# Twenty pairs of destinations per burst of counts, in a three-layer graph network on one core

## What is computed

```python
def _mean_agg(x, src, dst, n):
    msg_sum = segment_sum(x[src], dst, num_segments=n)
    cnt = segment_sum(ones, dst, num_segments=n)
    return msg_sum / maximum(cnt, 1.0)

def _sage_conv(x, src, dst, Wl, bl, Wr):
    return _mean_agg(x, src, dst, x.shape[0]) @ Wl.T + bl + x @ Wr.T

h = relu(_layernorm(x))
h = relu(_batch_norm(_sage_conv(h, src, dst, Wl0, bl0, Wr0), gamma0, beta0))
h = relu(_batch_norm(_sage_conv(h, src, dst, Wl1, bl1, Wr1), gamma1, beta1))
return x + log_softmax(_sage_conv(h, src, dst, Wl2, bl2, Wr2))
```

## Time and profile before

| | |
|---|---|
| median of 3 runs | 1584.37 us (1583.73 to 1584.45) |
| the profiled execution | 1584.4 us, span 1582.6 us |
| PE busy, share of the span | 1403.9 us (89%) |
| PEld busy | 1125.9 us (71%) |
| DVE busy | 559.7 us (35%) |
| ACT busy | 541.1 us (34%) |
| POOL busy | 639.2 us (40%) |
| block 0 of layer 0 | 0 to 63.5 us |
| blocks 1 to 24 of layer 0 | 63.5 to 545 us |

### The profile page before, as it was taken

How to read it: one execution, slowest core, us unless ns; L and a number is a source line. 1 busy time by engine, 2 the same in 40 slices (tenths; PEclk the granted TensorE clock), 3 DMA queues, 4 the chain that set the end, 5 groups by cost and what they waited for, 6 DMA issues and landing times. The chain is left out here.

```text
span 1582.6 us, 37175 instructions
## 1 busy us (share of the span) xinstructions
PE 1403.9 (89%) x16601; PEld 1125.9 (71%) x16601; DVE 559.7 (35%) x1023; ACT 541.1 (34%) x906; POOL 639.2 (40%) x636
## 2 busy tenths in 40 slices
PE   1499999999999999888988988988988898999997
PEld 0377777777777788666766766766766886788886
DVE  6968686868777632000010100001000211212223
ACT  4887878787877654000000000000000330000001
POOL 4332222222222000666566566566562004666640
PEclk9999999999999999999999999999999999999998
DMA  5254545454545427555555556455551367898992
GB/s 154 87 187 174 183 176 180 168 183 170 189 165 198 178 55 276 172 169 191 189 171 210 170 171 212 154 170 177 200 167 46 108 234 271 296 327 292 315 315 81
DMA packets 83896, 298.02 MB, mean 188 GB/s; under 512 B 17680, under 2 KB 53026, under 8 KB 70508
## 3 DMA queue, kind: packets, MB, share of 16 engines
q1 hardware_dynamic: 51900, 225.46, 39.8%
q0 software_dynamic: 25408, 65.24, 13.6%
q10 hardware_dynamic: 6424, 4.88, 1.0%
HBM read 204.30 MB, written 91.22 MB: 187 GB/s over the span
## 5 line engine op out<-in xcount | busy, mean ns | idle before, releaser
L1132 PE MATMUL bank<-ring,parts 128*128 128x250 f16 x6664 | 825.7, 274 | 41.3 <-issue 35.1
L1132 PEld LDWEIGHTS bank<-ring,parts 128*128 128x128 f16 x6664 | 624.5, 98 | 154.6 <-issue 65.2
L500 POOL DMA_INDIRECT hots<-table,src_i x518 | 492.9, 951 | 510.0 <-DMA table<-parts 204.1
L636 ACT CAST ring<-cells 128x980 f16<-128x980 f32 (+1 forms) x325 | 335.4, 1058 | 109.6 <-PE cells L1124 97.9
L1132 PE MATMUL cells<-ring,parts 128*128 128x250 f16 x1960 | 241.5, 276 | 27.4 <-issue 26.5
L864 DVE TENSOR_TENSOR hots<-iotas,tab 128x980 f16<-128x980 f16 (+3 forms) x262 | 245.4, 995 | 10.3 <-ACT tab L600 10.3
L1132 PEld LDWEIGHTS cells<-ring,parts 128*128 128x128 f16 x1960 | 190.2, 99 | 71.3 <-issue 49.2
L1669 ACT ACTIVATE Z<-bank,vec 128x250 f32<-128x250 f32 x48 | 20.0, 468 | 432.8 <-PE bank L1150 249.9
L1124 PEld LDWEIGHTS cells<-hots 64*128 64x128 f16 x4670 | 80.4, 96 | 95.6 <-issue 50.4
L1124 PE MATMUL cells<-hots 64*128 64x49 f16 x4670 | 107.2, 186 | 42.5 <-DVE hots L864 34.7
L452 POOL DMA_INDIRECT rows_i<-in_dst_rows_dram,row_i x25 | 36.3, 1453 | 192.4 <-DVE row_i L729 186.6
(11 more groups left out here) (199 smaller groups left out, 845.8 us busy)
## 6 DMA issues: line engine op xcount, KB each, us to landing
c_blocks<-ring SPq DMA_DIRECT2D x25, 3062.5 KB
ring<-c_blocks SPq DMA_DIRECT2D x39, 1562.5 KB
ring<-c_blocks SPq DMA_DIRECT2D x39, 1500.0 KB
rcb<-rc_row SPq DMA_DIRECT2D x68, 125.0 KB
hots<-table,src_i POOLq DMA_INDIRECT x518
Z<-in_x_dram SPq DMA_DIRECT2D x4, 768.0 KB, 7.5
table<-parts SPq DMA_DIRECT2D x2, 1536.0 KB
table<-parts ACTq DMA_DIRECT2D x2, 1536.0 KB
```

The source lines that it names most:

```text
L500: pool.indirect_dma_start(out=got[layer][:, 5 * (r % NGOT) + i, :], out_offset=None, in_=tables[layer], in_offset=bass.IndirectOffsetOnAxi ...
L636: act.copy(blk[c % 2][:, :, :].rearrange("p a (d g) -> p a d g", d=GD)[:, :, :, GPS * i:GPS * i + n], cells[t % 2][:, :, 0:n * NA].rearran ...
L1132: return pe.matmul(bank[b][:, 0:BD], view[0:r, a, part, m * P:m * P + P], blk[s][0:r, a, :], start=(a, part) == (0, 0), stop=(a, part) == ...
```

## The change

In `pe_layer0` the counts of two steps (i and i + 1, with i even) are issued in a run, 40 matmuls, ahead of all other work of the two steps; the sums of both steps follow, with the turns, the linear matmuls and the transposes at their places among them. The last step of a block stays alone. In `act_layer0` all of ScalarE's other work of a step moves into a function `act_chores(c, i)`, and is issued for both steps after the evictions of both. The work itself, the tiles, the semaphores and the lists of VectorE, GpSimd and SyncE are the same.

```diff
+        def act_chores(c, i):
+
+            t = NST * c + i
+            what, q, b = chores.get(t, ("", 0, 0))
...
+            if 1 <= c <= NG and i == 10:
+                a0, n, r = groups[c - 1]
+                w = (n - 1) * P + r
+                act.wait_ge(t_h0, c)
+                act.activation(Z[:, 0, P * a0:P * a0 + w], bank[7][:, 0:w], ACT.Relu).then_inc(a_h0, 1)
+
         def act_layer0():
...
                         act.copy(blk[c % 2][:, :, :].rearrange("p a (d g) -> p a d g", d=GD)[:, :, :, GPS * i:GPS * i + n],
                                  cells[t % 2][:, :, 0:n * NA].rearrange("p d (g a) -> p a d g", g=n)).then_inc(a_cells, 1)
-                    what, q, b = chores.get(t, ("", 0, 0))
...
-                        act.activation(Z[:, 0, P * a0:P * a0 + w], bank[7][:, 0:w], ACT.Relu).then_inc(a_h0, 1)
+                    if i % SPH == SPH - 1 or i == NST - 1:
+                        for k in range(i - i % SPH, i + 1):
+                            act_chores(c, k)
             act_last(0)
...
                 for i in range(NST):
                     t = NST * c + i
-                    if c < NB:
-                        pe_cells(c, i)
+                    if c < NB and i % SPH == 0:
+                        for k in range(i, min(i + SPH, NST)):
+                            pe_cells(c, k)
                     what, q, b = chores.get(t, ("", 0, 0))
                     if what == "turn":
                         pe_turn(q, b)
```

More of the change, by code:

```diff
@@ L619, in act_relu @@
             act.copy(small[0:r, a0:a0 + n, 0, :], X[0:r, a0:a0 + n, :]).then_inc(a_hi0, 1)
+        def act_chores(c, i):
+            t = NST * c + i
+            what, q, b = chores.get(t, ("", 0, 0))
+            if what == "sample":
+                act_sample(b)
+            elif what == "row":
+                act_row(q, b)
+            elif what == "turn":
+                act_turn(q, b)
+            if t == 1:
+                for b in range(*batches[1]):
+                    act_row(1, b)
+            elif t == 3:
+                act.wait_ge(v_lnvar, 1)
+                act.activation(rsx[:, 1, :], rsx[:, 2, :], ACT.Sqrt, bias=epsc[:, 0:1]).then_inc(a_lnstd, 1)
+            if t == TG - 24:
+                act.wait_ge(v_base, 1)
+                junk_wait()
+                act.activation(junk[0:W, 0:R], smp_i[0:W, :], ACT.Sign, bias=base[0:W, 4:5], scale=-1.0,
+                               accum_out=s1[0:W, NB:NB + 1]).then_inc(a_gsample, 1)
+                junked.append(a_gsample)
+            elif t == TG - 11:
+                act.wait_ge(d_grow, 16)
+                junk_wait()
+                act.activation(junk[0:W, 0:256], grow[0:W, :], ACT.Sign, bias=base[0:W, 4:5], scale=-1.0,
+                               accum_out=s2[0:W, NB:NB + 1]).then_inc(a_ginrow, 1)
+                junked.append(a_ginrow)
+            elif t == TG + 1:
+                act.wait_ge(d_gwin, 16)
+                act.activation(gloc[0:W, :], gloc[0:W, :].bitcast(I32), ACT.Identity,
+                               bias=base[0:W, 3:4]).then_inc(a_gconv, 1)
+            elif t == TG + 4:
+                act.copy(gsrc[0:W, :], gsrc[0:W, :].bitcast(I32)).then_inc(a_gconv, 1)
+            elif t in (TG + 8, TG + 11):
+                act_group_count((t - TG - 8) // 3)
+            if t in ln_at and ln_at[t] in act_groups:
+                act_relu(ln_at[t])
+            if c >= 2 and i == 6:
+                b = c - 2
+                act.wait_ge(t_lin, b + 1)
+                if b == 0:
+                    act.wait_ge(p_lo, len(act_groups))
+                    act.wait_ge(v_lo, len(vec_groups))
+                for m in range(2):
+                    act.activation(Z[:, m, BD * b:BD * b + BD], bank[7][:, BD * m:BD * m + BD], ACT.Identity,
+                                   bias=bias[0][:, m:m + 1]).then_inc(a_z, 1)
+            if 1 <= c <= NG and i == 10:
[3 more added lines that the diff above has]
+                act.activation(Z[:, 0, P * a0:P * a0 + w], bank[7][:, 0:w], ACT.Relu).then_inc(a_h0, 1)
@@ L637, in act_layer0 @@
                                  cells[t % 2][:, :, 0:n * NA].rearrange("p d (g a) -> p a d g", g=n)).then_inc(a_cells, 1)
-                    what, q, b = chores.get(t, ("", 0, 0))
-                    if what == "sample":
-                        act_sample(b)
-                    elif what == "row":
-                        act_row(q, b)
-                    elif what == "turn":
-                        act_turn(q, b)
-                    if t == 1:
-                        for b in range(*batches[1]):
-                            act_row(1, b)
-                    elif t == 3:
-                        act.wait_ge(v_lnvar, 1)
-                        act.activation(rsx[:, 1, :], rsx[:, 2, :], ACT.Sqrt, bias=epsc[:, 0:1]).then_inc(a_lnstd, 1)
@@ L682, in act_layer0 @@
-                    if 1 <= c <= NG and i == 10:
-                        a0, n, r = groups[c - 1]
-                        w = (n - 1) * P + r
-                        act.wait_ge(t_h0, c)
-                        act.activation(Z[:, 0, P * a0:P * a0 + w], bank[7][:, 0:w], ACT.Relu).then_inc(a_h0, 1)
+                    if i % SPH == SPH - 1 or i == NST - 1:
+                        for k in range(i - i % SPH, i + 1):
+                            act_chores(c, k)
             act_last(0)
```

31 lines of the change are left out of this document (removed).

## The result

The changed kernel takes 1591.69 us (median of 5 runs, 1586.92 to 1593.54) where the kernel before takes 1583.93 (5 runs beside it, 1582.31 to 1584.45): a ratio of 1.0046, 95% interval 1.0029 to 1.0063. It is slower by 7.8 us. The forecast was 1573.9, its range ended at 1586. The profiled execution of the changed kernel has 1591.69 us, its span 1589.8 us, so 7.2 us more than the span before, and a mean granted clock of 0.973, as before.

A forecast was written before the change was run, and what follows sets the result against it. TensorE was taken to bound blocks 1 to 24 of layer 0, ScalarE close behind. A saving of 31.3 us less 20.8 of added waiting left 10.5: 1584.4 - 10.5 = 1573.9 us, range 1560 to 1586.

The forecast's parts named there:

- x: Time of the second 20 count loads in a pair's run of 40 on TensorE: 0.26 us, bounded by 0.21 and 0.33.
- gross gain: TensorE's saving before new waits: 144 pairs at 0.20 us plus 23 gaps at 0.11 after linear matmuls, together 31.3 us.
- The rival with two gaps in a burst: The 0.21 us gap belongs to each step's own start, so nothing is saved and new waits are paid: 1595 us, chance 0.08.
- margin of a plain pair: With ScalarE doing evictions only, TensorE reaches the next burst's second half at 2.70 us, ScalarE frees it at 2.68: nothing lost.
- ScalarE sets the pace everywhere: Rival: evictions pitched at 1.06 us make every plain pair wait 0.07, 10 us in 144: 1584 us, chance 0.17.
- new waits: TensorE's added waiting, mainly for ScalarE's other work after its slack of 0.86 us is spent: 20.8 us in all.
- Turns: Step 11's turn waits for step 10's copy, now after both evictions: 0.9 to 1.3 us instead of 0.25, 0.9 more a batch.
- Samples: ScalarE's sample work at pair (10, 11), step 12 and pair (0, 1) makes TensorE wait 2.3 us, against 1.3 before.
- Rows: Row searches on ScalarE: covered when alone; two in pair (0, 1) make TensorE wait 0.55 us.
- The copy to Z: ScalarE's copy in each block makes TensorE wait 0.28 us, three times a batch 0.8; nothing before.
- The clock: Rival: longer waits drop TensorE's clock, costing 1.4 us a drop; one at each of fifteen places gives 1595 us, chance 0.07.
- ScalarE's lag: Rival: the lag is caught up elsewhere and only half of the added waiting comes: taken as 1562 us, chance 0.16.

The follow-up runs named there:

- e17: Kernel before, with evictions copying half their columns from block 2 on and the block store in seven column pieces; ratio 0.9927 to the kernel before.
- e18: Changed kernel, with evictions copying half their columns from block 2 on and the block store in seven column pieces; ratio 0.9762 to the kernel before.
- e13: Kernel before, with the block store in seven column pieces, one at each of steps 0 to 6 of the next block; ratio 0.9999 to the kernel before.
- e14: Changed kernel, with the block store in seven column pieces, one at each of steps 0 to 6 of the next block; ratio 0.9970 to the kernel before.
- e9: Kernel before, with blocks 1 to 24 storing only one of 49 column groups; ratio 0.9987 to the kernel before.
- e10: Changed kernel, with blocks 1 to 24 storing only one of 49 column groups; ratio 0.9957 to the kernel before.

## Why the prediction was wrong

The sum of what the change gives held. x, the second 20 loads, is 0.26 as taken (40 in 0.59 or 0.60), 15 sums take 1.51 (forecast 1.52), one gap of 0.21 stands for each pair, and plain pairs take 2.35 to 2.37 us where they do not wait. The gross gain is 27.5 to 30 us in e17 and e18 for 31.3. The rival with two gaps in a burst is refuted, and by the same rows the rule of the Trainium skill that a weight load is pulled ahead (TensorE: Matmul & The Clock Gate, on loading the stationary operand) does not cover this switch: 0.21 us stands at each pair, as it did at each step.

Two steps failed.

First, **the list of rivals had no place for TensorE's own instructions**. The prediction says "SyncE's, GpSimd's and VectorE's lists do not move" and that their work "costs nothing as long as TensorE is behind it", and looked at waits on semaphores only. Stops behind instruction packets grew by 18.4 us (1.4 to 19.8) and blocks 1 to 24 by 9.8, so the rest of the change gave 8.6. Where no stop is left it gives 3.8 (e13 and e14) or 5.3 (e9 and e10); the other 3 to 5 us must be waits that a stop took the place of, and only 2 of them are seen (26.0 us of waits for ScalarE against 28.1 in e14). The stops were in the trace of before, 1.4 us of them, and were passed by as noise. So was the margin, at n = 43 1.4 us between the late packet and TensorE. The Trainium skill's page Runtime: NRT & Kernel Launch, Instruction fetch mechanics, describes the blocks of 16 KiB, 256 instructions each, and calls the cost of crossing a boundary "mostly hidden"; the trace agrees on the 256, and has the cost hidden before, and not after. The Trainium skill's page DMA: Bandwidth & Descriptors, Queues, rings and completion order, says that a DMA engine goes round its queues by whole packets of some 9 to 17 descriptors. How many descriptors a row of the store makes no run shows; the trace has the instruction packet between two rows, after six of eight at 357.69, and not behind all of the engine's share.

Second, **the margin of a plain pair**. The step reads: "It comes there, at the second half of the next burst, at 2.37 + 0.33 = 2.70", against 2.68 for the eviction. But the same prediction had just taken 0.26 for the second 20 and so, by the same slope, for the first 20 of an unbroken run: the second half starts 0.26 after the first, at 2.63. The run of 40 that takes 0.67 in place of 0.59 is that wait. In e18 against e17 the median pair gains 0.20 or 0.21 at every place. In e14 against e13 it gains that only at step 6, behind the linear matmuls, and 0.14 at step 0, 0.12 at step 2, 0.08 at step 4, 0.14 at step 8; at step 10 it loses 0.07. The rival "ScalarE sets the pace everywhere" had the mechanism, with 0.17 for its chance and the wrong reason (an eviction's pitch of 1.06; it is 0.97: the row at 351.17 has two in 2.05). The Trainium skill's warning in TensorEngine Tiling (Array Packing), PSUM Bottleneck, is borne out: with evictions halved the pairs are worth 23.9 us, with whole ones 3.8.

The size of the new waits, forecast at 20.8 us, comes out at 31.3 - 3.8 = 27.5 with the stops away. It lies in the middle of the bursts: the 144 runs of 40 loads take 37.4 us more than 0.59 each in e14, and 3.6 in e18. A part of it has no term in the forecast at all: eight evictions of e14 and seven of the changed kernel start 0.46 to 0.50 us late with no releaser that the trace can name, and TensorE waits for them (0.86 us at 344.73 in the changed kernel); the cause is open. Turns had 0.9 to 1.3 us forecast at step 11's; in block 16 of the changed kernel it was 1.31, ScalarE's copy after both evictions just as described:

```profile
392.23 2.03 ACT L689 CAST ring<-cells 128x980 f16<-128x980 f32 x2
...
394.14 0.38 ACT L600 CAST tab<-bank 128x256 f16<-128x256 f32 x1
394.63 0.14 PEld L1108 LDWEIGHTS bank<-cf,parts 128*128 128x128 f32 x1 [1.31 <-issue]
```

Samples: 2.3 us forecast. The four waits of block 14 are 0.39 and 0.45 in the middle of two runs, and, by the rows below, 1.16 less the gap of 0.21, and 0.59 with the 0.07 by which loads of a run overlap: 2.45.

```profile
336.31 0.37 PEld L1131 LDWEIGHTS cells<-parts 64*128 64x128 f16 x20 [1.16 <-issue]
...
337.26 0.36 PEld L1131 LDWEIGHTS cells<-parts 64*128 64x128 f16 x20 [0.59 <-issue]
```

Rows: 0.55 forecast, 0.66 measured at 356.42. The copy to Z: 0.28 each forecast, nothing measured beyond the margin itself (in e14's blocks without searches the run of 40 behind the copy, at step 8, takes 0.66 to 0.68, and so does the one at step 2, which has no copy ahead of it).

The other rivals. The clock did not drop more than before: the mean granted clock is 0.973 in both. ScalarE's lag was not caught up. And the last sentence of the prediction listed what would make it wrong: "if plain pairs take over 2.45 us" did not come, and "if a run of 40 breaks in its middle without ACT as its reason" did come, as at 360.06, but not for the reason it was meant to tell of: the switch gain is real, and the cause that mattered was not on the list.

The forecast by its own sum was 1573.9. Add 6.7 for ScalarE, since the pairs give 3.8 us in e14 and not 10.5; add 13.6 for the whole store, with which they lose 9.8 and do not gain 3.8; take off the 2.6 that come back outside blocks 1 to 24: 1591.6, where 1591.69 was measured. The terms are differences of single traces, good to a microsecond or two.

## What to carry to other kernels

Look for idle time of an engine in the middle of a run of one operation, with no releaser, and see whether it comes at equal distances in instructions, matmuls and waits counted too (256 here): that is the instruction supply, and a large store on the same DMA engines can hold it up. Cut such a store into issues of about a microsecond, along the columns and not the partitions, before an order that speeds up TensorE is judged. And where a change spends slack, the time at which the second of two waits is reached has to be worked out from the new order's own rows, to the hundredth, if the margin is one of hundredths.

## What the runs showed of the hardware

- TensorE's instructions come in packets of 16,384 bytes, one for 256 of them (some 125 weight loads, as many matmuls, and the waits); TensorE went on 1.26 to 1.57 us after the end of a packet, mostly 2.20 to 2.45 us after its start, when it had stopped for one.
- A packet asked for near a store of 128 rows of 24,500 bytes (9.3 us) started, in 14 of the 16 cases in which TensorE stopped, 3.4 to 9.3 us after the store did, between rows as well as behind them. With the same store in seven column pieces no stop was left.
- A store of 32 partitions x 24,500 bytes took about 4 us, where 128 partitions took 7.8 to 10.0: a quarter of the bytes in about 0.42 of the time.
- The gap before 64-row weights that follow 128-row ones is 0.21 us whatever the order, and none stands on the way back.
- The kernel before took 1582 to 1592 us in four series of runs and 1455 to 1456 in two. Two of the series, 1592 and 1582 us, were on the same chip by its number. For the changed kernel, at 1592 and 1465 us, blocks 1 to 24 of layer 0 differed by 10 us (491.0 and 481.2), and most of the rest lies in layers 1 and 2 (1035.9 and 919.8 us behind block 24's last count).
